# Two graph attentions, a mixture of experts and a feed-forward chain: four pieces of work moved to other places or engines

## What is computed

```python
# layer 0, attention over the graph (4 heads of 64): x is standardized first
support = (xn @ weight).reshape(n, 4, 64)
logits  = f1[:, None, :] + f2[:, :, None]          # f1, f2: support times two vectors
neg     = where(adj != 0, leaky_relu(logits, 0.2) * adj, -inf)
x = x + softmax(neg) @ support + bias + xn @ proj_w.T + proj_b
# layer 0, experts: 2 of 16 per row
gate = xn @ gate_w + gate_b;  top 2, softmax;  x = x + layernorm(x + sum of two experts)
# layer 1, attention: scores need graph_bias * adj and a mask from the same matrix
scores = q @ k.T / 8 + graph_bias * adj;  scores = where(adj == 0, -1e9, scores)
x = x + softmax(scores) @ v @ Wout + bout
# layer 1, feed-forward: 30 steps of tanh, silu, layernorm, matmul
```

## Time and profile before

| | before |
|---|---|
| median of 3 runs | 2705.55 us (2704.66 to 2706.4) |
| the profiled execution, its own time | 2703.6 us |
| its span, first to last instruction | 2701.8 us |
| PE busy | 2479.9 us (92%) |
| DVE busy | 2001.9 us (74%) |
| ACT busy | 1611.9 us (60%) |
| POOL busy | 1419.9 us (53%) |
| mean granted TensorE clock | 0.954 |

### The profile page before, as it was taken

The page is one execution under the profiler, slowest core; times in us unless marked ns, Lnnn a source line. Parts: engine busy times, 40 slices in busy tenths (PEclk is TensorE's granted clock), DMA queues, the critical chain, the costliest instruction groups (busy, mean ns, idle before and its releaser), DMA issues. The chain is left out here.

```text
span 2701.8 us, 58198 instructions
## 1 busy us (share of the span) xinstructions
PE 2479.9 (92%) x20186; PEld 2029.4 (75%) x20187; DVE 2001.9 (74%) x4248; ACT 1611.9 (60%) x3039; POOL 1419.9 (53%) x1728
## 2 busy tenths in 40 slices
PE   6799999999976997188999999999599999999999
PEld 5377777777765997166777777777478888888888
DVE  5899999999925443887777777777667777777776
ACT  1577777777721332245666666666467777777775
POOL 6366676667342553522112211111388888888886
PEclk9799999999967999599999999999799999999999
DMA  2011111111063223201111111110000000000001
GB/s 100 21 43 44 62 42 43 52 54 43 22 221 137 70 70 94 102 7 42 43 41 41 41 42 60 42 41 21 7 1 0 0 0 0 0 0 0 0 0 41
DMA packets 43862, 114.01 MB, mean 42 GB/s; under 512 B 5621, under 2 KB 29918, under 8 KB 37982
## 3 DMA queue, kind: packets, MB, share of 16 engines
q1 hardware_dynamic: 38174, 97.16, 10.2%
q0 software_dynamic: 5568, 15.21, 1.8%
HBM read 99.21 MB, written 13.15 MB: 42 GB/s over the span
## 5 line engine op out<-in xcount | busy, mean ns | idle before, releaser
L2174 PE MATMUL f_pm<-f_wl,f_yt 128*128 128x256 f32 x2640 | 624.9, 380 | 0.0
L2174 PEld LDWEIGHTS f_pm<-f_wl,f_yt 128*128 128x128 f32 x2640 | 476.9, 191 | 51.5
L1101 POOL TENSOR_TENSOR ADJ<-ADJ,a_off 128x2708 f32<-128x2708 f32 x22 | 131.3, 5967 | 542.8 <-DVE ADJ L1180 542.8
L119 POOL TENSOR_SCALAR f_yy<-f_th,f_rs 128x255 f32<-128x255 f32 x660 | 367.9, 573 | 21.8 <-POOL f_rs L114 21.8
L2024 DVE SCALAR_TENSOR_TENSOR f_gg<-f_th,f_pm 128x512 f32<-128x512 f32 x319 | 218.9, 686 | 177.4 <-ACT f_th L2118 177.2
L529 ACT COPY a_wt<-a_tp 128x512 f32<-128x512 f32 x528 | 256.5, 566 | 146.7 <-PE a_tp L744 146.6
L552 POOL TENSOR_SCALAR a_off<-ADJ 128x677 bf16<-128x677 f32 x84 | 284.3, 3407 | 76.2 <-DMA ADJ<-in_adj 61.8
L629 DVE SCALAR_TENSOR_TENSOR a_lg<-a_f1s,F2S,a_fo 128x1024 f32<-128x1024 f32 (+1 forms) x264 | 296.4, 1151 | 29.4 <-PE a_fo L731 28.1
L1160 DVE CUSTOM_DVE_ANT_0 a_sc<-a_qk,ADJ 128x1024 f32<-128x1024 f32 (+1 forms) x264 | 288.1, 1092 | 31.0 <-PE a_qk L1258 30.7
L2118 ACT ACTIVATE f_th<-f_pm 128x512 f32<-128x512 f32 x319 | 190.6, 597 | 200.3 <-PE f_pm L2174 200.3
L1124 ACT ACTIVATE a_sc<-a_sc,a_mx 128x1024 f32<-128x1024 f32 (+1 forms) x264 | 277.7, 1052 | 45.1 <-DVE a_mx L1165 45.1
(11 more groups left out here) (308 smaller groups left out, 4535.0 us busy)
## 6 DMA issues: line engine op xcount, KB each, us to landing
ADJ<-in_adj SPq DMA_DIRECT2D x44, 1354.0 KB, 5.8
W<-in_L_ffn_w SPq DMA_DIRECT2D x32, 512.0 KB, 9.3
m_got<-YD SPq DMA_DIRECT2D x6, 768.0 KB, 10.6
out<-X SPq DMA_DIRECT2D x21, 128.0 KB
X<-in_x SPq DMA_DIRECT2D x3, 768.0 KB, 10.2
XD<-XF SPq DMA_DIRECT2D x3, 768.0 KB
m_b<-in_L_ffn_b SPq DMA_DIRECT2D x1, 2048.0 KB, 7.8
m_rows<-XD,SLOT POOLq DMA_INDIRECT x58, 2.8
```

The lines of the kernel that those rows point to most:

```text
L119: return eng.tensor_scalar(out, x, rs[:, 0, bass.ds(t, 1)], rs[:, 1, bass.ds(t, 1)], ALU.mult, ALU.add)
L2174: mm = pe.matmul(out, yt[:, g, r, k, :], wl[:, k, :], start=(k == 0), stop=(k == KD - 1))
```

## The change

Four pieces. First, in `layer0_prepare` x arrives in batches of 2, 6, 8 and 5 tiles plus the last one, with proj_w and the biases loaded right behind the first two tiles; DVE takes the moments of the first 8 tiles, and those of the other 14 in between the `results` of the first tiles, two at a time; the selector tables are made behind tile 11 and the two row tables behind tiles 13 and 15; the loop over `results` is unrolled. Second, POOL makes the first tile's mask at the end of `layer0_prepare`, and does its subtraction at the head of `layer0_attention`; DVE's two pieces are gone. Third, the gate weight and bias are loaded at the head of `layer0_attention`, into a buffer that later holds b1 of the experts; PE in `moe_route` waits for these two alone. Fourth, in `layer1_prepare` graph_bias is loaded too, and DVE makes the mask of the first adjacency tile and scales and adds it in one instruction, between the moments and the first `results`; in `layer1_attention` DVE starts with the scores, and the second tile's mask and scaling stand behind the first head. PE there waits for Wout only after the first nine score chunks.

```diff
+ARRIVALS = [(0, 1), (1, 4), (4, 8), (8, NPAIR)]
...
-            for k, (a, end) in enumerate(BATCHES):
+            for k, (a, end) in enumerate(ARRIVALS):
                 s0, s1 = 2 * a, min(2 * end, NT - 1)
                 sp.dma_start(X[:, s0:s1, :], io["x"][P * s0:P * s1, :].rearrange("(t p) d -> p t d", p=P)
                              ).then_inc(x_in[k], 16)
+                if k == 0:
+                    sp.dma_start(pw[:, :, :], io["L0_gnn_proj_w"].rearrange("(k p) o -> p k o", p=P)).then_inc(w_in, 16)
+                    sp.dma_start(bias[:, 0, :], io["L0_gnn_bias"].to_broadcast([P, D])).then_inc(w_in, 16)
+                    sp.dma_start(bias[:, 1, :], bcast_rows(io["L0_gnn_proj_b"], P)).then_inc(w_in, 16)
             sp.dma_start(X[:, NT - 1, :], io["x"][LAST:N, :]).then_inc(x_in[-1], 16)
-            sp.dma_start(pw[:, :, :], io["L0_gnn_proj_w"].rearrange("(k p) o -> p k o", p=P)).then_inc(w_in, 16)
-            sp.dma_start(bias[:, 0, :], io["L0_gnn_bias"].to_broadcast([P, D])).then_inc(w_in, 16)
-            sp.dma_start(bias[:, 1, :], bcast_rows(io["L0_gnn_proj_b"], P)).then_inc(w_in, 16)
...
+            pool.wait_ge(keep["adj_in"][0], 16)
+            for cols in QUARTERS:
+                pool.tensor_scalar(keep["OFF0"][:, 0, cols], keep["ADJ0"][:, 0, cols], 0.0, HUGE, ALU.is_equal,
+                                   ALU.mult).then_inc(keep["off_done"][0], 1)
...
+            def row_stats(t):
+
+                k = next(k for k, (a, end) in enumerate(ARRIVALS) if 2 * a <= t < 2 * end)
+                a, end = ARRIVALS[k]
+                if t == 2 * a:
+                    dve.wait_ge(x_in[k], 32 if end == NPAIR else 16)
+                dve.bn_stats(st[:, t, :], X[:, t, :]).then_inc(stats, 1)
+                if t == 2 * end - 1:
+                    dve.wait_ge(stats, 2 * end)
+                    row_moments(dve, st, mom, 2 * a, 2 * end, folded, 3 * k).then_inc(moments, 1)
+            for t in range(2 * ARRIVALS[1][1]):
+                row_stats(t)
+
+            def selectors():
...
-            slot_moments(dve, X, st, mom, stats, folded, moments,
-                         [(s, 32 if s is x_in[-1] else 16) for s in x_in])
...
-            slot_pairs(dve, results)
+            for t in range(NT):
+                results(t // 2, t % 2)
+                for u in range(2 * (ARRIVALS[1][1] + t), 2 * (ARRIVALS[1][1] + t + 1)):
+                    if u < NT:
+                        row_stats(u)
+                if t == NT // 2:
+                    selectors()
+                elif t in (NT // 2 + 2, NT // 2 + 4):
+                    first_rows((t - NT // 2) // 2 - 1)
...
+            gate = keep["GATE"]
+            sp.dma_start(gate[:, 0:KD * E].rearrange("p (k e) -> p k e", k=KD),
+                         io["L0_ffn_gate_w"].rearrange("(k p) e -> p k e", p=P)).then_inc(keep["gate_in"], 16)
+            sp.dma_start(gate[:, KD * E:(KD + 1) * E], bcast_rows(io["L0_ffn_gate_b"], P)).then_inc(keep["gate_in"], 16)
...
+            for k, cols in enumerate(QUARTERS):
+                pool.wait_ge(off_done[0], k + 1)
+                pool.tensor_tensor(adj[:, 0, cols], adj[:, 0, cols], off[:, 0, cols],
+                                   ALU.subtract).then_inc(adj_done[0], 1)
...
-            quarters = [slice(k * N // parts, (k + 1) * N // parts) for k in range(parts)]
-            dve.wait_ge(adj_in[0], 16)
-            for cols in quarters:
-                dve.tensor_scalar(off[:, 0, cols], adj[:, 0, cols], 0.0, HUGE, ALU.is_equal,
-                                  ALU.mult).then_inc(off_done[0], 1)
             table(1, 2 * NC)
-            dve.wait_ge(off_done[0], parts)
-            for cols in quarters:
-                dve.tensor_tensor(adj[:, 0, cols], adj[:, 0, cols], off[:, 0, cols], ALU.subtract).then_inc(adj_done[0], 1)
...
-            first_adj(sp, io, layer1["ADJ1"], layer1["adj_in"])
+            sp.dma_start(gb[:, :], io["L1_gnn_graph_bias"].rearrange("a b c -> (a b) c").to_broadcast([P, 1])
+                         ).then_inc(gb_in, 16)
+            first_adj(sp, io, adj, adj_in)
...
+            dve.wait_ge(adj_in[0], 16)
+            dve.tensor_scalar(off[:, :], adj[:, 0, :], 0.0, MASKED, ALU.is_equal, ALU.mult).then_inc(off_done, 1)
+            dve.wait_ge(gb_in, 16)
+            dve.wait_ge(off_done, 1)
+            dve.scalar_tensor_tensor(adj[:, 0, :], adj[:, 0, :], gb[:, :], off[:, :], ALU.mult,
+                                     ALU.add).then_inc(bias_done[0], 1)
...
-                bias(0, b)
-            pool.wait_ge(w_in, 32)
+            bias(0, 1)
+            pool.wait_ge(bout_in, 16)
...
-            dve.wait_ge(gb_in, 16)
-            for b in range(2):
-                off_tile(0, b)
-                scale_tile(0, b)
             for h in range(3):
                 for c in range(NC):
                     score((0, 0, h), c)
+                if h == 0:
+                    off_tile(0, 1)
+                    scale_tile(0, 1)
...
-            pe.wait_ge(w_in, 32)
             for h in range(3):
                 for c in range(NC):
                     scores((0, 0, h), c)
+            pe.wait_ge(wout_in, 16)
...
-            pe.wait_ge(w_in, 48)
+            pe.wait_ge(gate_in, 32)
...
-        b1 = ph.sb("b1", [P, E * FB])
+        b1 = keep["GATE"]
```

95 lines of the change are left out of this document (48 added, 47 removed).

## The result

| | before | after |
|---|---|---|
| median | 2705.41 us (4 runs, 2704.66 to 2706.4) | 2682.1 us (4 runs, 2679.94 to 2685.11) |
| span of the profiled execution | 2701.8 us | 2680.2 us |
| mean granted TensorE clock | 0.954 | 0.958 |

The ratio is 0.9913, with a 95% interval of 0.9901 to 0.9926. Predicted were 2684.5 us, within 2677 to 2692. The spans differ by 21.6 us. A stage's length is taken from its first instruction to the first of the next in the timeline. With the changed kernel's stages beside those of before, the differences are: first stage 76.95 to 69.45 (-7.5), first attention 688.17 to 685.86 (-2.3), routing 74.27 to 70.89 (-3.4), experts 230.63 to 232.65 (+2.0), combining 58.59 to 58.31 (-0.3), preparing 78.99 to 80.48 (+1.5), second attention 719.20 to 709.48 (-9.7), last stage 775.00 to 773.08 (-1.9).

A forecast was written before the change was run, and what follows sets the result against it. TensorE was taken to bound the steady attention loops, so only openings between stages count: -7.0 - 1.7 - 3.6 + 1.4 - 10.1 = -21.0 us, from 2703.6 to 2682.6, plus 1.95 for the median: 2684.5, range 2677 to 2692.

The forecast's parts named there:

- First stage: -7.0 predicted: First stage: first standardized tile 7.2 us earlier, at 14.1 instead of 21.30, less 0.2 us of stall; net 7.0 us gained.
- the margin of 0.3 us at the third tile: First stage's opening: GpSimd has the third tile ready at 19.7, TensorE's third transposition is due at 20.0.
- the ninth tile: First stage, the tight one: standardized at 31.5, wanted by TensorE at 31.8; 0.2 us of stall taken.
- the rival of the locked ports: First stage's end and under the multiply-add: VectorE and GpSimd block each other on shared ports; +6 us, 2690.5, chance 0.08.
- The row that the sum went by: First attention's opening before: VectorE's four mask pieces, 2.33 us, run inside one GpSimd quarter, so they wait little.
- First attention: -1.7: First attention's opening: VectorE loses mask work, TensorE's first table chunk comes 0.45 us sooner, then 1.2 more; bounds -0.4 and -3.7.
- The rival "slower": First attention: GpSimd's mask quarters slow further in the buffer's new place; at 4700 ns +33 us, 2717; chance 0.04.
- Routing: -3.6: Routing's opening: TensorE waits for GpSimd's second tile, ready at 769.3, instead of a load; 3.6 us won, bounds -2 and -5.8.
- the third rival: Routing: TensorE's clock stays up and its eleven pairs would halve; -12 us, 2672.5, chance 0.05.
- Preparing stage: +1.4: Preparing stage: mask and multiply-add ahead of VectorE's first results make TensorE's next v product slip 1.4 us; bounds 0 and +2.7.
- VectorE, with 0.45 idle a pair, catches up: Preparing stage after the v product's slip: VectorE's 0.45 us idle a pair lets it catch up, the slip staying at 1.4.
- Second attention: -10.1: Second attention's opening: first score waits only for TensorE's first chunk, nine scores end at 1224.6 against 1234.80; bounds -8 and -11.9.

The follow-up runs named there:

- e11: The changed kernel run once more, unaltered; median 2680.06 us, ratio 0.9907 to the kernel before.
- e6: Changed kernel with both first adjacency tiles of the second attention prepared in the preparing stage, ScalarE scaling, GpSimd adding both masks; median 2690.91 us.
- e2: Kernel before with only the early load of gate weights and bias, in a buffer shared with the experts' first bias; median 2701.39 us, ratio 0.9987.
- e3: Kernel before with only the second attention's part: first adjacency tile masked, scaled and added by VectorE in the preparing stage; median 2699.07 us, ratio 0.9976.
- e5: Kernel before with one VectorE memset cut into 35, so 34 more instructions on VectorE and nothing else; median 2702.83 us, ratio 0.9991.
- e1: Kernel before with only the first stage's new order (x batches, moments, weave); the first mask stays with VectorE in the attention; median 2692.71 us.
- e4: Changed kernel with the first attention's first mask and its subtraction back on VectorE in that attention's opening; median 2686.94 us.
- e12: e4 with one VectorE memset at its start cut into 57, so everything behind it on VectorE stands 56 instructions later; median 2684.45 us.
- e8: Changed kernel with the experts' first two tiles of rows gathered into the output buffer; experts' stage 236.08 us, against 232.65 in the changed kernel.
- e9: e8 with VectorE's wait for the big bias load moved from its third weight staging to the first sum that reads it; median 2681.17 us.
- e7: Changed kernel with the prepared adjacency tile's multiply-add cut in three and put behind VectorE's third, sixth and ninth pair of results; median 2681.19 us.
- e10: e9 with the second adjacency tile's mask (VectorE) and scaling (ScalarE) in the preparing stage too, GpSimd's addition staying in the attention; median 2680.52 us.

## Why the prediction was right, term by term

The prediction was right in sum and in sign, and no term of it that had a price was more than 1 us off. Part of the closeness is luck: in the first stage a gain that was larger than forecast hides a cost that was set at nothing, and two further stages moved by +2.0 and -1.9 us and cancel. By medians the change gained 23.3 us (25.1 in e11 and its own before), 21.0 being forecast. Means over the profiles of the table stand beside the terms.

**First stage: -7.0 predicted.** The seven profiles with both parts of the change in it (the changed kernel and e6 to e11) have 70.24 us in the mean, the four without the new order (before, e2, e3, e5) 77.38: -7.1. That is two things that cancel in part. With the new order but no mask on GpSimd (e1, e4, e12) it is 69.46, so the order gives -7.9. The first tile came at 12.66 and not at 14.1: u and v landed 1.3 us sooner than in before (VectorE's products start at 6.43, not 7.73), and a statistic cost 0.37. The prediction had left u and v where they were; yet in all ten profiles with the new order of loads the products start at 6.43 to 7.09, in the four without it at 7.66 to 8.00. Of the margin of 0.3 us at the third tile nothing was left in this profile, TensorE waited 0.18 us there, because VectorE itself waited 1.37 us for the second batch of x; in e6 to e11 that wait is nil. At the ninth tile there was none.

**The mask beside VectorE.** The remaining 0.8 is GpSimd's mask, which the prediction set at nothing: 0.89 and 0.67 us for a cast and a subtraction that take 0.35 and 0.34 without it, shown by e4 and e12. So the rival of the locked ports was right in kind at this place, at 0.87 us instead of its +6, and e6 shows its full form. The row that the sum went by, four VectorE mask pieces inside a GpSimd quarter, was misread, for it is a sum over four. One by one, in the timeline of before:

```profile
77.05 2.86 POOL L552 TENSOR_SCALAR a_off<-ADJ 128x677 bf16<-128x677 f32 x1 [14.45 <-POOLq L58]
77.41 1.06 DVE L697 TENSOR_SCALAR a_off<-ADJ 128x677 bf16<-128x677 f32 x1
78.39 0.50 DVE L697 TENSOR_SCALAR a_off<-ADJ 128x677 bf16<-128x677 f32 x1
79.88 2.48 POOL L552 TENSOR_SCALAR a_off<-ADJ 128x677 bf16<-128x677 f32 x1
85.47 1.41 DVE L702 TENSOR_TENSOR ADJ<-ADJ,a_off 128x677 f32<-128x677 f32 x1
```

One mask piece took 1.06 us and the other three 0.50 to 0.52, the GpSimd quarter beside them 2.86 and the next 2.48, and of the four subtractions one took 1.41 and the others 0.85 to 0.87. So the waits of half a microsecond were there to be seen before the change. Which instruction waits is open: of the three casts beside GpSimd's mask only one did.

The Trainium skill ("SBUF — State Buffer", section "SBUF: two separate sides") says that the shared pair is held for a whole instruction by whichever starts first, GpSimd's or a VectorE operation in a two-port fast mode or with two SBUF inputs. The copy of e6, which waited for all of GpSimd's 5.92 us, agrees with it. Beside the mask's quarters of 2.5 us the waits were 0.33 to 0.55 us, and a subtraction with two SBUF inputs ran inside a quarter (62.85 in the changed kernel) in its usual 0.34; that the rule does not give, and the measurement decides.

**First attention: -1.7.** 686.74 in the mean of the seven with GpSimd's mask, 688.07 in the mean of the seven without: -1.3, within the bounds. Together with the 0.8 above, this part of the change is worth 0.5 us by stages. By medians e4 and e12 are 2.4 to 6.9 us above the changed kernel; gaps and a longer last stage, which the edit does not touch, stand beside it there, so what the part is worth as a whole stays open within these bounds. The rival "slower" is out: the quarters took 3384 ns in the mean, against 3407 before.

**Routing: -3.6.** 70.90 in ten profiles, 74.14 in four: -3.2. The second transposition had to wait for GpSimd's tile until 760.07, 4.8 us after the stage's start and not 4.2. The tile was begun where the prediction had it, but took 1.19 us (758.83 to 760.01), in before 1.19 as well; the prediction took 0.65, the mean of the row's six, which hides that the first is the long one. The clock stayed at 0.50 there, so the third rival is out.

**Preparing stage: +1.4.** 80.47 in the six profiles with the change's form and no gaps (the changed kernel, e3, e8, e9, e11, e12), 78.97 in the three of before's form and no gaps (before, e2, e5): +1.5. The number was right, its reason only in part. The slip of the second v product is there (1.76), but e7 takes it away and the stage is no shorter: VectorE's sum of work ends the stage. "VectorE, with 0.45 idle a pair, catches up" was the sentence that failed.

**Second attention: -10.1.** 709.16 against 719.20: -10.0. The first score came 2.06 us after the stage's start (1.9 taken, where the row named, 1.06 for two, makes 2.1), and the sum of parts held.

**The two stages set at nothing.** That they would not move was wrong, twice by about 2 us, with opposite signs. The last stage's -1.9 holds 1.3 to 1.5 us of gaps ahead of its first statistics: shown by e5, which changes nothing but where VectorE's instructions stand. That a late supply of instructions makes these gaps is argued and not shown; the traces show only that they go with the place. What is left, up to 3 us between kernels with the same head, builds up evenly over the stage and stays open. The experts' +2.0 goes with the clock: in the six profiles where it did not fall again the stage took 230.6 to 231.3, in the eight others, where TensorE stood still for 1.97 us or more and the clock fell, 232.5 to 236.1. The pause alone doesn't decide it: e5 had 1.96 us and no fall, e10 1.97 us and a fall. Every longer pause was followed by a fall. What the fall costs is seen in e4 and e5, which are alike up to it: TensorE turns to the third tile 12.36 and 12.35 us after the stage's start, behind pauses of 2.14 and 1.96 us. The stretches behind, of e4 and then of e5, with the clock third from the end:

```profile
843.10:846.50 3.40, 3.40 (x13) 3.00 (x12) 1.54 (x4) 0.00 (x0) 0.55 (x1) 0.50 0.15 39
```

```profile
852.00:856.00 4.00, 2.73 (x15) 2.29 (x16) 1.13 (x3) 0.05 (x1) 0.95 (x1) 1.00 0.22 78
```

The fourth tile's turn comes at 18.60 in e4 and at 16.93 in e5, 1.67 us apart, and so far apart are the two stages as well (232.46 and 230.79). So of the changed kernel's +2.0 some 1.7 is the fall, and the rest is the third tile, which came 0.25 us later than in before. An earlier high clock gives nothing back here, for the rows of the third tile set its start, 12.15 to 13.9 us after the stage's start in the eleven profiles without e8's edit, however early the high clock came. Why the high clock came anywhere from 7.4 to 11.0 us after the stage's start is open. The Trainium skill ("TensorE: Matmul & The Clock Gate", Part 1) says that the gate's watch runs free of the program, so that one kernel meets it in different phases; these runs agree with that and can't show it.

## What to carry to other kernels

In a kernel whose loops are filled by one engine, price the openings: take the last wait, then the next one behind it, and the sum holds to a microsecond. A mask or a copy that is moved to GpSimd is not free by itself: look at what VectorE does beside it, one instruction at a time. A merged row or a mean hides the one that waited (0.50, 1.06, 0.50, 0.50) and the one that was long (1.19 ahead of five of 0.56 to 0.58). Before a difference of one or two microseconds is credited to an edit, compare stage by stage, and look in stages that the edit doesn't touch for gaps put down to "issue" and for a granted clock that fell.
